# First two chunks' expert rows gathered within the experts' program, and the value buffer's zeros narrowed and moved behind the first chunk's sums

## The reference

```
logits = x @ w_router.T;  _, top_idx = top_k(logits, 1)
scores = sigmoid(logits) * one_hot(top_idx, 16)
gate, up = split(einsum('eth,ehf->etf', scores.T[:, :, None] * x, gate_up_proj))
expert_out = einsum('etf,efh->eth', up * silu(gate), down_proj)
shared = silu(x @ w_gate.T) * (x @ w_up.T) @ w_down.T
x = layernorm(x + shared + expert_out.sum(axis=0))
q, k, v = x @ wq + bq, x @ wk + bk, x @ wv + bv        # layer 1, then rope on q and k
```

## Time and profile before

| | us |
|---|---|
| median of 3 runs | 1492.09 |
| lowest, highest | 1489.83, 1494.17 |
| the profiled execution, device time | 1491.71 |
| its span, first to last instruction | 1489.7 |

### The profile page before, as it was taken

The page is one execution under the profiler, slowest core; times in us unless marked ns, Lnnn a source line. Parts: engine busy times, 40 slices in busy tenths (PEclk is TensorE's granted clock), DMA queues, the critical chain, the costliest instruction groups (busy, mean ns, idle before and its releaser), DMA issues. The chain is left out here.

```text
span 1489.7 us, 24886 instructions
## 1 busy us (share of the span) xinstructions
PE 1368.9 (92%) x9358; PEld 761.6 (51%) x9358; DVE 1062.0 (71%) x2351; ACT 774.5 (52%) x1066; POOL 322.9 (22%) x407
## 2 busy tenths in 40 slices
PE   6897899989999989858998889999999999999996
PEld 3565578856898877423345422333333333333285
DVE  4887466661121128878994798999999999997077
ACT  2344266621111102326664315787888888888754
POOL 3110322243000017743335440000000000000011
PEclk9999799999999999959999968999999999999999
DMA  9548533356988842774421650333222343220001
GB/s 340 194 139 245 166 122 128 124 171 228 299 274 300 278 143 80 222 216 123 134 76 42 187 171 2 77 98 91 68 67 68 80 100 86 68 67 2 1 1 57
DMA packets 152841, 198.68 MB, mean 133 GB/s; under 512 B 15723, under 2 KB 124799, under 8 KB 152594
## 3 DMA queue, kind: packets, MB, share of 16 engines
q1 hardware_dynamic: 141004, 165.34, 36.9%
q0 software_dynamic: 9200, 29.64, 6.5%
q10 hardware_dynamic: 2518, 2.13, 0.5%
HBM read 136.08 MB, written 60.70 MB: 132 GB/s over the span
## 5 line engine op out<-in xcount | busy, mean ns | idle before, releaser
L2139 DVE TENSOR_REDUCE xa_part<-psum 128x1 f32<-128x512 f32 (+1 forms) x768 | 462.6, 661 | 20.5 <-PE psum L1992 18.6
L2091 ACT ACTIVATE xa_P<-psum 128x1024 f32<-128x1024 f32 (+1 forms) x416 | 403.5, 1020 | 105.4 <-PE psum L2016 104.7
L2016 PE MATMUL psum<-sa_Q,xa_K 48*128 48x512 bf16 (+3 forms) x1664 | 268.1, 382 | 3.9 <-DMA sa_Q<-xa_mrow 2.9
L1992 PE MATMUL psum<-xa_K,sa_Q 48*128 48x512 bf16 (+1 forms) x768 | 239.4, 388 | 4.9 <-DVE xa_part L2139 1.5
L2032 PE MATMUL psum<-xa_P,xa_V 128*32 128x512 f32 (+1 forms) x1664 | 223.5, 609 | 0.4 <-ACT xa_P L2091 0.4
L1992 PEld LDWEIGHTS psum<-xa_K,sa_Q 48*128 48x128 bf16 x768 | 59.3, 94 | 232.1 <-DVE xa_part L2139 160.6
L2016 PEld LDWEIGHTS psum<-sa_Q,xa_K 48*128 48x128 bf16 (+3 forms) x1664 | 105.7, 97 | 69.5 <-ACT xa_P L2091 21.2
L2136 DVE CUSTOM_DVE_ANT_0 psum<-psum,cf_sb 128x512 f32<-128x512 f32 (+3 forms) x256 | 119.4, 521 | 19.3 <-PE psum L1992 18.6
L1334 PEld LDWEIGHTS psum<-xtT,wgu 128*128 128x128 f32 x992 | 115.5, 192 | 5.8 <-issue 4.6
L1334 PE MATMUL psum<-xtT,wgu 128*128 128x128 f32 x992 | 115.9, 275 | 1.4 <-issue 0.8
L2091 ACT ACTIVATE sa_P<-psum 128x1024 f32<-128x1024 f32 (+3 forms) x128 | 83.4, 702 | 43.3 <-PE psum L2016 43.1
(11 more groups left out here) (245 smaller groups left out, 2126.2 us busy)
## 6 DMA issues: line engine op xcount, KB each, us to landing
wgu<-in_f_gu SPq DMA_DIRECT2D x31, 1024.0 KB
xa_K<-kx SPq DMA_DIRECT2D x192, 100.1 KB, 5.0
wdn<-in_f_dn SPq DMA_DIRECT2D x31, 512.0 KB
vx<-xv_v SPq DMA_DIRECT2D x48, 256.0 KB, 3.4
xa_V<-vx POOLq DMA_DIRECT2D x16, 768.0 KB, 6.5
sa_Q<-qs SPq DMA_DIRECT2D x64, 96.0 KB, 2.3
sa_K<-ks SPq DMA_DIRECT2D x64, 96.0 KB, 2.4
sa_Q<-qx SPq DMA_DIRECT2D x64, 96.0 KB, 2.3
```

The costliest lines, as they stand in the source:

```text
L1992: last = pe.matmul(out[:, 0:width], hb.q(u)[tile:tile + HALF, to, qt * P:(qt + 1) * P], hb.k(u)[tile:tile + HALF, to, cut[e]:cut[e] + widt ...
L2016: last = pe.matmul(out(j), hb.k(u)[tile:tile + depth, to, kt * P:kt * P + r], hb.q(u)[tile:tile + depth, to, q0(kt):L], start=(half == 0), ...
L2091: act.activation(Pr[0:r, (u * KT + kt) % PR, h:h + 2, 0:w_], S_PS(p)[0:r, :, 0:w_], ACT.Exp, scale=SCALE).then_inc(s_exp, 1)
L2139: dve.tensor_reduce(part[:, g % 2, col + qt, e:e + 1], src[:, 0:cut[e + 1] - cut[e]], AX, ALU.max).then_inc(s_1free, 1)
```

## The change

Four of the 16 gathers, those of chunks 0 and 1, move from the head of POOL's list in the combining program to the end of POOL's list in the experts' program, behind the wait for the last stores. Their semaphores `s_ga` are allocated earlier and kept. The zeroing of the value buffer writes only the 15 words of each head that stay zero, and it moves, with the ones, behind chunk 0's sums and statistics in DVE's list.

```
 # Values.init
-        v = self.v[:, :, :, :].rearrange("p u k n -> p (u k n)")
-        engine.memset(v, 0.0).then_inc(self.s_zero, 1)
+        v = self.v[:, :, :, :].rearrange("p u k (h w) -> p (u k h) w", w=VW)
+        engine.memset(v[:, :, HD + 1:VW], 0.0).then_inc(self.s_zero, 1)
         engine.wait_ge(self.s_zero, 1)
-        engine.memset(v.rearrange("p (h w) -> p h w", w=VW)[:, :, HD:HD + 1], 1.0).then_inc(self.s_ones, 1)
+        engine.memset(v[:, :, HD:HD + 1], 1.0).then_inc(self.s_ones, 1)
 # l0_ffn
+        s_ga = [sem(f"f_ga{c}", keep=True) for c in range(CHUNKS)]
...
                     for u in range(R):
                         pool.wait_ge(s_yo[u], 16 * ((ETILES - u + R - 1) // R))
+                    for c in range(DONE):
+                        gather(env, pool, c, xs, slot, s_ga)
...
+def gather(env, pool, c, xs, slot, s_ga):
+    for t in PAIR_TILES(c):
+        pool.indirect_dma_start(out=xs[:, t, :], out_offset=None, in_=env.yg,
+                                in_offset=bass.IndirectOffsetOnAxis(ap=slot[:, t:t + 1], axis=0)).then_inc(s_ga[c], 16)
 # combine_and_prepare, POOL
-                for c in range(AHEAD):
-                    gather(c)
+                for c in range(DONE, AHEAD):
+                    gather(env, pool, c, xs, slot, s_ga)
 # combine_and_prepare, DVE
-                val.init(dve)
                 for c in range(STEPS):
+                    if c == 1:
+                        val.init(dve)
```

More of the change, by code:

```diff
@@ L1500, in l0_ffn, with combine_and_prepare @@
         env.next_layer()
-        return combine_and_prepare(nc, env, hT, xs, slot, hb)
-def combine_and_prepare(nc, env, hT, xs, slot, hb):
+        return combine_and_prepare(nc, env, hT, xs, slot, s_ga, hb)
+def gather(env, pool, c, xs, slot, s_ga):
+    for t in PAIR_TILES(c):
+        pool.indirect_dma_start(out=xs[:, t, :], out_offset=None, in_=env.yg,
+                                in_offset=bass.IndirectOffsetOnAxis(ap=slot[:, t:t + 1], axis=0)).then_inc(s_ga[c], 16)
+def combine_and_prepare(nc, env, hT, xs, slot, s_ga, hb):
     w, PS = env.w, env.PS
@@ L1523, in combine_and_prepare @@
         s_all = sem("f_all")
-        s_ga = [sem(f"f_ga{c}", keep=True) for c in range(CHUNKS)]
         def bias(n):
@@ L1568, in _ @@
                     if c + AHEAD < CHUNKS:
-                        gather(c + AHEAD)
+                        gather(env, pool, c + AHEAD, xs, slot, s_ga)
                     for n in blocks_at(c):
```

## The result

The changed kernel takes 1495.38 us (median of 8 runs, 1493.61 to 1496.79) against 1492.22 us before (8 runs of the same sessions): ratio 1.0023, 95% interval 1.0014 to 1.0032. So it is slower by about 3 us, within the 0.3% that the prediction counted as no change. Forecast: 1495.0 us.

The account below looks back on a forecast made before the run. Bound: a chain of PE's last matmul or POOL's DRAIN, barrier, zeroing, DVE's sums and statistics, transposes. Barrier 5.25 us later less 2.3 on DVE gives 2.95; 1492.09 + 2.95 = 1495.0 us, range 1490.6 to 1497.2.

Parts of the forecast that it names:

- no change: Whole kernel: differences within about 0.3% (4.5 us) can't be told from none; chance of same 0.83.
- The barrier: Experts' program's end: gathers end at 555.2 us, DRAIN adds 3.9, so it opens 5.25 us later.
- the two prices: Four gathers on POOL: 5.55 us counted from the release, or 4.82 from the first row's start; the longer was taken.
- the last 0.3: POOL's DRAINs: four more DMAs add 0.3 us at the experts' end and take 0.3 from the combining program's end.
- The 0.08 for each DMA: POOL's DRAIN: from 16 to 47 DMAs it grows by some 0.08 us for each.
- DVE's chain: Combining program's start, release to end of first dve_apply: 10.58 us becomes 8.28 with narrowed, moved zeroing, gain 2.3 us.
- One step: Combining program's start: nobody waited for the four gathers, so their removal is worth nothing on DVE.
- the sum: At chunk 0's transposes: 5.25 us later, less 2.3 given back on DVE, makes 2.95 us later.
- A short DRAIN: Rival at the experts' end: 0.1 us of DRAIN gives 1491.2 us, 1.4 us gives 1492.5; chance 0.25.
- The DRAIN behind the landing: Rival at the experts' end: DRAIN starts only when gathers have landed, total +4.8 us, 1496.9 us; chance 0.12.
- PE's clock: Rival: the clock falls in PE's new rest before the transposes, 16 matmuls take 5.54 us, total 1496.9; chance 0.06.

Follow-up runs that it names:

- the runs with 51 and 78: 51: changed kernel with POOL waiting for its four gathers' landing, 1497.3 us; 78: kernel before with each expert-row store issued as two DMAs, 1495.8 us.
- Zeros only: Changed kernel with all gathers back in the combining program, only the zeroing narrowed and moved: 1494.4 us, ratio 1.0013 to the kernel before.
- gathers alone: Changed kernel with the zeroing as before, only the four gathers moved: 1498.0 us, ratio 1.0037 to the kernel before.
- one chunk early: Changed kernel with only chunk 0's two gathers in the experts' program and an extra POOL DRAIN behind the 28th store: 1491.1 us, ratio 0.9999 to before.
- zeros on ACT: Kernel before with value-buffer zeros and ones written by ACT and an extra POOL DRAIN behind the combining program's last gather: 1495.0 us, ratio 1.0020.
- the DRAIN in the combining program alone: Kernel before with only one more POOL DRAIN, behind its last gather in the combining program: 1491.2 us, ratio 1.0001.

## Why the prediction was right

**The barrier: right, and its closeness in part luck.** Forecast 5.25 us late, measured 5.1. The mechanism is the forecast one: the gathers, priced by spacing and not by their own durations, outlast PE, and the DRAIN comes behind them. But two terms were off and nearly cancelled. From the first gather's start to the end of the fourth it was 4.83 us, the 4.82 of before; of the two prices I had taken the longer, 5.55, and the gathers ended 0.9 us behind PE's last matmul instead of 1.4. The DRAIN ran its own 4.2 us behind them, 3.9 and four times 0.082. I had left the last 0.3 out against an equal gain at the combining program's end; that gain is there (the DRAIN ends 1.0 us behind POOL's last instruction instead of 1.4). The 0.08 for each DMA was read from 16 and 47 DMAs alone, past the row with 32 and 1.55 us, which doesn't fit it; the runs with 51 and 78 bore it out for this program's DMAs.

**DVE's chain: right in size.** Forecast gain 2.3 us; measured from barrier to transposes 11.45 before and 9.12 after, 2.33. The MEMSET's row says 1.66 us, but from the end of the statistics (563.77) to its end (565.77) it is 2.00 us, the forecast's 2.02. By the Trainium skill (VectorE: DVE Perf Modes, section Zero memsets can be issued as uint32 (trn2)) a memset takes one cycle per element, an estimate of 2.0 us for 1920 at the 0.96 GHz that it gives for the engine. The time between the neighbours agrees with it, the row doesn't.

**One step was wrong, and the sum didn't show it.** The prediction said of the removed gathers that nobody waited for them and that on DVE's chain their removal was worth nothing. Zeros only showed what was next: without the zeroing ahead of it the first add waits 4.08 us for the rows. The 2.3 us can be had only because the rows are there already. So the parts don't add: gathers alone cost 6.0 us at the program's end, zeros alone 3.4, both together 2.9. The sum came out since I computed the chain with both in place, and without having asked when the rows are ready: that they were is luck. Where the zeroing was the whole change, I did forecast a gain of 2.3 us, and the kernel got slower.

**The rivals.** A short DRAIN is out. The DRAIN behind the landing was half right: part of a DRAIN's work does come behind the last landing, about 0.04 us for each DMA in the table above, but not the whole of it. In the changed kernel the landing was at 557.66, and the full 3.9 us counted from there would have ended at 561.6 instead of 560.02. PE's clock didn't fall in the new rest of 2.33 us in the changed kernel, but after one of 2.1 us with one chunk early it did, so that rival was closer than its 0.06 (its sum, +4.87 us, makes 1497.0 and not 1496.9).

**What stays open:** why 32 POOL DMAs cost 1.55 us in another program, whether a DRAIN really does half of its work behind the last landing, and what of a change of one or two us survives in later programs. With zeros on ACT the stage ends 1.5 us later than before and the median is 3.4 us higher; with the DRAIN in the combining program alone the stage ends 1.5 us earlier and the median is the same.

## What to carry to other kernels

A program's end can have a price on POOL that no instruction of the kernel shows: here its DRAIN took 0.08 us for each store, scatter or gather that POOL had issued since the last one, and it also ended behind the landing of what was in flight. Read that DRAIN's row before you put DMAs in front of it, and put them there only if POOL is early by that much, or let POOL execute a DRAIN earlier, where it waits anyway, and look at what stands behind it. Before taking covering work out of a chain, write down when everything that it covered is ready; the next latest thing sets the gain.

## What the runs showed of the hardware

- A DRAIN on POOL: 3.905 us with 47 DMAs issued before it, 4.232 with 51, 6.437 with 78, all landed and POOL idle; but 1.55 us with 32 in another program. With a DMA in flight it ended 0.2 us (5 DMAs), 0.9 us (20), 1.9 us (44) and 2.4 us (51) behind the last landing. An early one resets the count: behind it the DRAIN at the combining program's end finished about 0.1 us behind POOL's last instruction instead of 1.4.
- A MEMSET's row begins late: 1.66 us in the row, 2.00 us between its neighbours, for 1920 elements.
- A rest of PE of 2.33 us left the full clock in place in one kernel (mean 1.00 from 567.0 to 569.3 and behind it), a rest of 2.1 us in another was followed by a mean of 0.57. In the second PE had come back from the barrier after only 2.2 us, and its clock had fallen while it worked. Why the two differ isn't shown.
